# Second attention of a two-layer gated transformer: context keys and values from split fp32r products, in a new order of steps

## The reference

```python
x = x + tanh(g_xattn[0]) * L0_xattn(layernorm(x), ctx_768, ...)     # 8 heads, first attention
x = x + tanh(g_ffn[0]) * L0_ffn(layernorm(x), ...)                  # 8 experts, top 2
x = x + tanh(g_xattn[1]) * L1_xattn(ctx_768, layernorm(x), mask, ...)
x = x + tanh(g_ffn[1]) * L1_ffn(layernorm(x), ...)                  # 16 experts, top 4

def L1_xattn(x, latents, mask, ...):         # x: 32 x 361 x 192 context, latents: 32 x 100 x 256
    xn = layernorm(x, ln_x_g, ln_x_b)
    ln = layernorm(latents, ln_l_g, ln_l_b)
    q = ln @ Wq.T
    kv = concatenate([xn @ Wkv.T, ln @ Wlkv.T], axis=1)   # 256 key and 256 value columns
    qn = rmsnorm(q, qn_g) * SCALE ; kn = rmsnorm(k, kn_g) # per head, 4 heads of 64
    attn = softmax(where(mask, qn @ kn.T, -max))
    return (attn @ v) @ Wo.T + bo
```

## Time and profile before

| | us |
|---|---|
| median of 3 runs | 2028.29 (2022.79 to 2030.18) |
| the profiled execution, its own time | 2024.5 |
| its span | 2022.7 |
| span busy: TensorE matmul | 1878.4 (93%) |
| span busy: VectorE | 1362.8 (67%) |
| span busy: GpSimd | 1075.3 (53%) |
| span busy: ScalarE | 1053.8 (52%) |
| mean granted TensorE clock | 0.964 |

### The profile page before, as it was taken

One profiled execution on the slowest core, in us unless ns is written; L12 is line 12 of the kernel. 1 busy time (PEld: TensorE's weight loads), 2 busy tenths in 40 slices (PEclk: granted clock), 3 DMA queues, 4 the chain that ended last, 5 costly groups with the idle time before them and its releaser, 6 DMA issues. The chain is left out here.

```text
span 2022.7 us, 41825 instructions
## 1 busy us (share of the span) xinstructions
PE 1878.4 (93%) x11917; PEld 1379.8 (68%) x11917; DVE 1362.8 (67%) x4364; ACT 1053.8 (52%) x2664; POOL 1075.3 (53%) x1246
## 2 busy tenths in 40 slices
PE   5999999999999389999969999999999849999997
PEld 4888888888887278888835555555555536777665
DVE  4788888888887633322237787878888656666665
ACT  2554555454544323333238877887888733444443
POOL 2444445444444344554445777777777633555555
PEclk9999999999999589999979999999999959999999
DMA  4121111111115223333311211121111954555654
GB/s 140 50 56 30 42 28 42 29 42 29 42 30 208 74 40 53 53 51 51 54 35 32 58 52 54 50 58 54 56 48 56 300 194 86 97 93 93 98 93 67
DMA packets 138416, 142.35 MB, mean 70 GB/s; under 512 B 31658, under 2 KB 128658, under 8 KB 137816
## 3 DMA queue, kind: packets, MB, share of 16 engines
q1 hardware_dynamic: 98586, 92.90, 15.6%
q0 software_dynamic: 37888, 44.51, 13.8%
q10 hardware_dynamic: 1726, 2.28, 0.4%
HBM read 89.88 MB, written 51.94 MB: 70 GB/s over the span
## 5 line engine op out<-in xcount | busy, mean ns | idle before, releaser
L1956 POOL DMA_INDIRECT out<-y,xr x115 | 178.1, 1549 | 179.5 <-DVE y L1994 107.5
L925 POOL TENSOR_SCALAR prob<-prob,rc 100x363 f32<-100x363 f32 x256 | 147.4, 586 | 176.1 <-DVE rc L739 173.2
L634 ACT ACTIVATE prob<-psS,nm 100x361 f32<-100x361 f32 x256 | 141.4, 562 | 78.8 <-DVE nm L734 78.8
L1149 PE MATMUL psJ<-wkv,cTn 96*121 96x512 f32 x384 | 177.7, 600 | 0.0
L1692 POOL DMA_INDIRECT acc<-y,slots x57 | 90.4, 1585 | 136.8 <-DVE y L1750 121.9
L1609 POOL DMA_INDIRECT rows<-row,pos_of x128 | 134.5, 1051 | 44.1 <-issue 34.5
L1727 DVE TENSOR_TENSOR hid<-psU,gate 128x512 f32<-128x512 f32 x57 | 39.4, 692 | 159.6 <-PE psU L1844 159.6
L1594 POOL TENSOR_TENSOR rk<-rk,neghalf 121x12 f32<-121x12 f32 x64 | 127.0, 1985 | 5.3
L734 DVE TENSOR_REDUCE nm<-psS 100x2 f32<-100x722 f32 x128 | 115.9, 906 | 16.2 <-PE psS L523 8.1
L1978 DVE TENSOR_TENSOR pre<-psG,late 128x512 f32<-128x512 f32 x115 | 79.6, 692 | 68.2 <-PE psG L2082 68.1
L2038 ACT ACTIVATE x_hi<-psX 128x128 fp32r<-128x128 f32 x115 | 31.9, 277 | 179.0 <-PE psX L2069 179.0
(11 more groups left out here) (330 smaller groups left out, 5574.6 us busy)
## 6 DMA issues: line engine op xcount, KB each, us to landing
xr<-rows SPq DMA_DIRECT2D x115, 136.5 KB, 2.4
expert_w<-in_L_ffn_moe_w SPq DMA_DIRECT2D x8, 1024.0 KB, 15.5
late<-in_ctx SPq DMA_DIRECT2D x32, 181.5 KB
cT<-in_ctxT SPq DMA_DIRECT2D x32, 180.5 KB, 2.9
cT<-in_ctxT SPq DMA_DIRECT2D x64, 90.2 KB, 2.9
expert_w<-in_L_ffn_moe_w SPq DMA_DIRECT2D x8, 512.0 KB, 6.8
expert_w<-in_L_ffn_W1T SPq DMA_DIRECT2D x16, 256.0 KB, 6.5
expert_w<-in_L_ffn_W3T SPq DMA_DIRECT2D x16, 256.0 KB, 6.7
```

The lines of the kernel that those rows point to most:

```text
L634: s.activation(prob[:, q, 0:S], psS[0:N, h, 0:S], ACT.Exp, bias=nm[:, q:q + 1], accum_out=rs[:, q:q + 1]).then_inc(exp_done, 1)
L925: g.tensor_scalar(prob[:, q, :], prob[:, q, :], rc[:, q:q + 1], 1.0, ALU.mult, ALU.mult).then_inc(prob_done, 1)
L1149: mm = t.matmul(ph[0:rows, 0:cols], lhs, wt[:, k, :], start=k == 0, stop=k == 1)
L1956: g.indirect_dma_start(acc, bass.IndirectOffsetOnAxis(row_token[:, j % RING, :], 0), y[:, j % 4, :], None, compute_op=ALU.add).then_inc(sc ...
```

## The change

The keys and values of the context are computed from parts. ScalarE rounds the weights (`wkv_hi`) and each batch's normalised, transposed context (`c_hi`) to fp32r; the remainders are `wkv_lo` and, for the context, `c_ends` and the upper half of `c_hi`'s second row block. A chunk then takes five fp32r matmuls of 512 columns in place of two float32 ones. The 192 channels are stored as two overlapping blocks of 128 partitions (channels 0 to 127 and 64 to 191), so `ctx_transpose` takes 128 columns, `cTn` has 128 partitions, and the constants and `wkv1` are loaded that way.

The split parts of the weights and context lie where eight of the sixteen W2 expert matrices go, so those are loaded later (`load_late_w2_1`), when all keys and values are done. The steps of all four engines come in a new order, with a new `PROJECTIONS`, and `y_rank` is no longer one pass later on TensorE.

```diff
-        cTn = sb("cTn", [CK, 2, SP])
+        cTn = sb("cTn", [P, 2, SP])
+        wkv_hi = nc.alloc_sbuf_tensor_at("wkv_hi", [P, 2, 2 * I1], F32R, offset=taken)
...
+                    if i == B - 2:
+                        s.wait_ge(kv_mm, len(QKV) * B)
+                        load_late_w2_1(s, a, c)
...
-                        t.wait_ge(ct_out, 2 * b + 2)
+                        t.wait_ge(kv_low, 2 * b + 3)
+                        cols = slice((j - 2) * CH, (j - 1) * CH)
+                        hi, ends, rest = c_hi[:, 0, cols], c_ends[:, cols], c_hi[:, 1, cols]
+                        t.matmul(ph[0:CH, :], hi, wkv_hi[:, 0, :], start=True, stop=False)
+                        t.matmul(ph[0:CH, :], hi, wkv_lo[:, 0, :], start=False, stop=False)
+                        t.matmul(ph[0:CH, :], ends, wkv_ends[:, :], start=False, stop=False)
+                        t.matmul(ph[0:CH, :], rest, wkv_hi[:, 1, :], start=False, stop=False)
+                        t.matmul(ph[0:CH, :], rest, wkv_lo[:, 1, :], start=False, stop=True).then_inc(kv_mm, 1)
...
+                def ctx_high(b):
+                    s.wait_ge(ct_out, 2 * b + 2)
+                    if b >= 1:
+                        s.wait_ge(kv_mm, len(QKV) * b)
+                    s.activation(c_hi[:, :, 0:SP], cTn[:, :, :], ACT.Copy).then_inc(kv_high, 1)
...
+                s.activation(wkv_hi[:, :, :], c["wkv1"][:, :, :], ACT.Copy).then_inc(kv_high, 1)
+                s.activation(wkv_ends[0:CR, :], c["wkv1"][0:CR, 0, :], ACT.Copy)
+                s.activation(wkv_ends[CR:P, :], c["wkv1"][CR:P, 1, :], ACT.Copy).then_inc(kv_high, 1)
...
+                def ctx_low(b):
+                    v.wait_ge(kv_high, b + 3)
+                    v.tensor_tensor(c_ends[0:CR, 0:SP], cTn[0:CR, 0, :], c_hi[0:CR, 0, 0:SP].bitcast(F32), ALU.subtract)
+                    v.tensor_tensor(c_ends[CR:P, 0:SP], cTn[CR:P, 1, :], c_hi[CR:P, 1, 0:SP].bitcast(F32), ALU.subtract).then_inc(kv_low, 1)
...
+                v.wait_ge(kv_high, 2)
+                v.tensor_tensor(wkv_lo[:, :, :], c["wkv1"][:, :, :], wkv_hi[:, :, :].bitcast(F32), ALU.subtract).then_inc(kv_low, 1)
...
+                def ctx_mid(b):
+                    g.wait_ge(kv_high, b + 3)
+                    g.tensor_tensor(c_hi[0:CR, 1, 0:SP], cTn[0:CR, 1, :], c_hi[0:CR, 1, 0:SP].bitcast(F32), ALU.subtract).then_inc(kv_low, 1)
...
-                    at(i - 1, values, 1)
-                    at(i, scores, 1)
-                    at(i - 1, y_out)
+                    at(i - 1, values, 1)
+                    at(i - 1, y_out)
+                    at(i + 2, qkv, 1)
```

More of the change, by code:

```diff
@@ L213, in load_attention1 @@
             s.dma_start(c["qk_g"][r, 1:2], a["L1_xattn_kn_g"].rearrange("(p k) -> p k", k=1)).then_inc(loaded, 16)
+    for k, first in ((0, 0), (1, C - P)):
+        s.dma_start(c["wkv1"][:, k, :], a["L1_xattn_WkvT"][first:first + P]).then_inc(loaded, 16)
     for n, src, p in ATTENTION1:
@@ L1031, in attention1 @@
         QKV = ("q", "kv0", "kv1", "kv2", "kv3")
[L1032 to L1035, removed]
+        KV_ORDER, CT_ORDER = ("kv0", "q", "kv1", "kv3", "kv2"), ("ct0", "ct1")
+        PROJECTIONS = ((2, "lt"), (2, "ct1"), (2, "kv0"), (1, "qt"), (1, "kt0"), (2, "q"), (1, "kt1"), (2, "kv1"), (2, "kv3"), (2, "kv2"), (3, "ct0"))
+        uses = [(i + ahead, use) for i in range(-3, B + 1) for ahead, use in PROJECTIONS if 0 <= i + ahead < B]
         def bank(b, use):
@@ L1509, in _ @@
                     v.memset(c["base"][:, e:e + 1], float(e * REGION))
-                for i in range(-4, B + 2):
-                    at(i, maxes, 1)
-                    at(i + 3, ctx_stats)
-                    at(i - 1, y_norm)
-                    at(i + 3, x_norm)
-                    at(i + 4, x_stats)
+                v.wait_ge(kv_high, 2)
+                v.tensor_tensor(wkv_lo[:, :, :], c["wkv1"][:, :, :], wkv_hi[:, :, :].bitcast(F32), ALU.subtract).then_inc(kv_low, 1)
+                for i in range(-4, B + 1):
+                    at(i + 3, ctx_norm)
                     at(i, reciprocals, 1)
-                    at(i - 2, route_weights)
-                    at(i + 3, ctx_norm)
-                    at(i - 1, route_groups)
+                    at(i - 1, route_top)
                     at(i + 2, sum_squares, 0, 3, sqA, ssA)
-                    at(i - 1, route_top)
-                    at(i + 2, sum_squares, 3, 5, sqB, ssB)
                     at(i + 1, maxes, 0)
                     at(i - 1, y_dispatch)
+                    at(i + 3, x_norm)
+                    at(i + 2, sum_squares, 3, 5, sqB, ssB)
+                    at(i + 1, maxes, 1)
+                    at(i + 1, reciprocals, 0)
+                    at(i + 4, ctx_stats)
+                    at(i, y_add)
                     at(i + 2, rms_scale, 1, 3, rkA, knA)
                     at(i + 2, rms_scale, 3, 5, rkB, knB)
-                    at(i, y_add)
-                    at(i + 1, reciprocals, 0)
+                    at(i, y_norm)
+                    at(i - 1, route_weights)
+                    at(i + 3, ctx_low)
+                    at(i + 4, x_stats)
+                    at(i, route_groups)
                 steps = Count(plan)
```

106 lines of the change are left out of this document (62 added, 44 removed).

## The result

The changed kernel takes 2014.22 us (median of 5 runs, 2009.81 to 2018.81), the kernel before beside it 2028.51: a ratio of 0.9934, with a 95% interval of 0.9912 to 0.9957. It is faster, but by 14 us where 45 were forecast, and the time lies above the range of 1962 to 2010. The profiled execution has a span of 2012.7 us, against 2022.7. So 10.0 us lie between the two traces, and they can be placed by four events in each, the prediction's own: TensorE's first matmul on a context chunk (L1149 before, L1170 now) and its last (L1149, L1174), the last logits (`sc`), and the first transposes of the second experts (`psX`).

A forecast was written before the change was run, and what follows sets the result against it. TensorE was taken to pace an 18.1 us pass, VectorE the new 16.7 us one. Over 31 passes -43.4, start +1.5, drain -3: -44.9 us, from a median of 2028.3 to 1983 us; range 1962 to 2010.

The forecast's parts named there:

- TensorE's chunks: Context chunks on TensorE: five fp32r matmuls take 1.22 us a chunk with loads hidden, saving 1.72 us a pass.
- E: Rival, context chunks on TensorE: each of 15 matmuls pays its load in series, pass about 19.0, 2056 us; chance 0.01.
- ScalarE's busy time: ScalarE's list in the second attention: 14.8 us plus 0.8 for `ctx_high`, 15.6 us a pass, hidden beside VectorE.
- the 0.05 for the signal: TensorE's new stall at `y_out` waiting for `oT`: 0.37 us plus an estimated 0.05 for the signal, 0.42 a pass.
- 0.72 to 2.0: Bounds in us for GpSimd's new subtraction `ctx_mid`, taken as 1.0; at 2.0 GpSimd would set a pass of 17.3.
- The drain: From the last context chunk to the last logits: 3 us less, bounds -6 and +3, half at the lower clock.
- D: Rival: TensorE's clock drops to 1.2 GHz for part of each pass, 2084 us at a share of 0.2; chance 0.04.
- The late W2 loads: Eight 256 KB loads issued after all chunks: costed at nothing, up to 7 us without cover.
- the first and largest step: VectorE's list gains `ctx_low`, two subtractions at 0.534 us each, +1.07, so 16.5 us, the longest list and the pass.
- the second step: Stretch from the last logits to the experts: no term of its own, so 0 us.
- C: Rival: earlier waits come back elsewhere, pass 17.8 to 18.3, time 2028 within 10 us; chance 0.05.
- B: Rival: hand-offs between engines set the pass, or `ctx_mid` nears 2 us; pass 17.0 to 17.7; chance 0.27.

The follow-up runs named there:

- the run on VectorE alone: Changed kernel with both subtractions for the context's low parts on VectorE and none on GpSimd; 1987.09 us, ratio 0.9818 to the kernel before.
- The single instructions: Changed kernel plus a block behind its end running single VectorE and GpSimd instructions alone, then together; GpSimd's addition took 1.76 us for 1.26, whole time not meaningful.
- the split products: Changed kernel with every engine's steps in the order of the kernel before, keeping the five fp32r matmuls a chunk; 2027.96 us, ratio 1.0014 to before.

## Why the prediction was right and wrong

**Right.** TensorE's chunks take 1.14 to 1.26 us (0.91 to 1.03 from the first start to the fifth, and 0.23 for the fifth) for 1.22, so loads hide and E is out. ScalarE's busy time is 0.873 x 17.92 = 15.6 a pass, as forecast, and TensorE's 0.915 x 17.92 = 16.4. VectorE is the longest list and sets the pass. `ctx_high` takes 0.81. `y_out` waits 0.35 for `oT` where 0.42 was forecast, so the 0.05 for the signal, which no run shows, was not needed. `ctx_mid` took 1.18, inside 0.72 to 2.0. The drain fell by 2.8 us for 3, though more than the half that the prediction names was at the lower clock before (0.50 from 1615 to 1648, 33 of 48 us). The granted clock is 1.00 in the middle of the stage, so D is out. The late W2 loads, issued at 1588, hold up nothing that the trace shows. The direction is right.

**Wrong, the first and largest step**: "VectorE's list gains ctx_low ... +1.07, so 16.5 us". The step put the price of two instructions that run beside `ctx_mid` at that of the same instruction alone, and put at nothing what GpSimd's new list does to the rest of VectorE's. The duration came from L709, an instance that ran undisturbed, and the first subtraction here and both in the run on VectorE alone do take 0.53. The sum failed because durations do not add when GpSimd gets new work beside them. By the changed kernel's rows, against before (L1372 386 ns, the two small ones 180 and 168): L1420 +0.54, `ctx_norm` 3 x 0.128 = +0.38, L1483 +0.17 (it ends at 1206.04, beside a scatter that runs from 1204.92 to 1206.07), L1495 +0.17, two others -0.09, and the wait for the held-up root +0.48. 16.53 + 1.65 = 18.18, 0.26 over the measured 17.92, which these rows don't explain: some of them overlap, and a few others got shorter by up to 0.03. By the busy shares the sum closes: VectorE's busy time rose from 0.802 x 18.11 = 14.53 us a pass to 0.924 x 17.92 = 16.56, 2.03 more where 1.07 was forecast, and 15.46 + 2.03 + 0.48 = 17.97. The pass was forecast 1.4 us shorter and got 0.19 shorter. I had seen the possibility, but on one side only: the bound of 2.0 us for `ctx_mid` spoke of "a read of two large tensors beside VectorE's", and VectorE's own price had no such bound.

The Trainium skill, "SBUF — State Buffer", section "Who interferes with whom", states the mechanism: VectorE and GpSimd share one pair of ports as an exclusive lock, and a VectorE instruction with two SBUF inputs contends with a GpSimd instruction that reads SBUF; casts and `tensor_scalar` can contend too. The single instructions agree (1.76 for 1.26 us, 1.59 for 0.55, nothing on reductions). By that page `ctx_mid` beside `ctx_low` was a clash to be priced before the run. It also says that whoever issues first gets the pair; VectorE's `tensor_scalar` of 1.59 us was issued no later than GpSimd's addition and waited all the same.

**Wrong, the second step**: the stretch from the last logits to the experts was not costed, that is, put at nothing; "It keeps its steps" was true of the attention's chain and said nothing of GpSimd's scatters, whose order the change also moves. It costs 6.8 us, and 6.5 of it come back with another order.

**The range.** Its middle, 1983, was added up from the median of before (2028.3), its two ends from the profiled execution (2024.5). From the median the upper end would be 2014.3, and the measured 2014.2 would lie just inside. That would have been luck: the pass of 17.92 us lies outside the 16.3 to 17.6 either way.

**The rivals.** C named the right pass, 17.8 to 18.3, at a chance of 0.05, though not its cause (waits that come back elsewhere) and not the time (2028 within 10; measured 14 less). It was turned down because "every list ends 1.6 us or more under 18.1"; that was the same wrong VectorE list. B's mechanism isn't that of the changed kernel, where VectorE waits 0.48 us a pass in all, but hand-offs are what the split products wait for in the old order.

## What to carry to other kernels

Before work is given to GpSimd to relieve VectorE, list for each new SBUF-reading instruction what VectorE does beside it. In the runs here reductions, batch statistics, the reciprocal and the subtraction with one operand in PSUM kept their time; additions and subtractions of two SBUF tensors, casts and `tensor_scalar` waited for the end of GpSimd's instruction, however small they were, or made GpSimd's wait for theirs, and `tensor_scalar` was slower beside a memset too (0.83 us for 0.55). Where VectorE set the pace, a subtraction on VectorE (0.53 us) was cheaper than the same on GpSimd, which took 1.18 there and cost VectorE 0.54. When an order of steps is changed, read the last passes too: what follows may wait for the one queue that was put last.

## What the runs showed of the hardware

The two engines exclude each other by whole instructions: a copy of two columns took 0.50 us for 0.17 beside `mask`, and ended with it. GpSimd's indirect DMA is held up as well: 3.70 and 5.58 us for 0.99, beside VectorE's subtractions of 128 x 2048 with both inputs in SBUF, and 0.99 in the run that issues it ahead of them. The passes repeat within 0.03 us in most runs, so an edit of 0.2 us a pass is read from the intervals where the whole time can't show it: in the first `y_add` alone, ahead of which nearly nothing differs, the profiled runs differ by up to 12 us (1069.6 to 1081.5).
